# The second attention of a two-layer transformer kernel with another softmax path, another order of its steps, and batch 15's weighing shared by two engines

## The chip, the cores and the metric

One core of one Trainium2 chip runs the whole program in one launch. The metric is the device time of that launch in microseconds (us). The engines are PE (TensorE: matmuls and transposes, results to PSUM), DVE (VectorE), ACT (ScalarE), POOL (GpSimd) and SP (SyncE, which here issues DMAs).

## The reference

16 batches of 100 tokens, 512 features. Two layers, each a cross-attention and a feed-forward part, every one behind a layer norm and added to its input. The change touches only the second layer's attention and the layer norm behind it:

```python
def _L1_xattn_ref(q, latent_kv, Wq, Wkv_expand, Wout):      # 16 heads of 32
    qp = q @ Wq.T
    k, v = jnp.split(latent_kv @ Wkv_expand.T, 2, axis=-1)  # latent_kv: 100 rows, 128 wide
    scores = einsum('bhqd,bhkd->bhqk', qh, kh) / sqrt(32)
    scores = where(tril, scores, lowest)                     # causal
    attn = softmax(scores, axis=-1)
    return (einsum('bhqk,bhkd->bhqd', attn, vh) -> [b, q, 512]) @ Wout.T

x = x + _L1_xattn_ref(_layernorm(x), ctx, ...)
x = x + _L1_ffn_ref(_layernorm(x), ...)                      # 32 experts, 8 chosen per token
```

The expert part reads the normed rows twice: as transposed halves for the gate's logits, and from a table in DRAM out of which tokens are gathered.

## The kernel before, in words

The program runs stage by stage: first attention, first feed-forward part, second attention (`attention1`), routing, experts. Products keep float32 accuracy by splitting each operand into a float16 high part (written by ACT) and the rest (a float16 low part, written by DVE), and summing three products; so nearly every PSUM tile is read by ACT, then by DVE, and only then is its bank free.

`attention1` is written out by hand, engine by engine, as a loop over steps `s` (`LAST` = 22). Step `s` scores batch `s` (16 heads of 100 x 100, in four PSUM banks `sbank`, one for each head group `j`; a group is the four heads 4m + j), and finishes batch `b = s - 2`: transpose of its probabilities (`turn`, line 1880), their split (`probs_high` on ACT, line 2018, `probs_low` on DVE, line 2178), and their product with the values (`values`, line 1893). Beside it run the projections for coming batches (`project_v`, `project_qk`, line 1831, four batches or a *chunk* at a time), the output projection of a finished chunk (`output`, line 1831 with `aT`,`w_o`), its transpose back to rows (`output_rows`, line 1909), its addition to `x` (`add_rows`, line 2194), the next layer norm (`moments` line 187, `before_root`, `root` on ACT line 240, `after_root`, `norm_row` line 247, `norm_turn` line 1917, `norm_high` line 2044, `norm_low` line 2206), the rows for the gather table (`row_high` on ACT, line 2040, `row_low` on POOL, line 2108, a DMA from SP, line 1815, through two buffers) and the gate's `logit_sums`. `choose` (from line 2243) waits for the last of these.

The softmax of batch `s`: DVE takes the maxima of all 16 heads from PSUM (`peaks`, line 2154, 1600 columns) and scales them (line 2157). For three of the four head groups ACT takes exp head by head, with the maximum as bias, and sums as it goes (line 2012, 12 instructions, each with one that reads the sum). For the fourth group DVE adds the maxima itself (`shift`, line 2163), ACT takes one exp of 400 columns (line 2008), DVE sums it (line 2170). DVE inverts the totals (line 2173), POOL multiplies all 1600 probabilities (`normalise`, line 2102). The scores of the next batch may overwrite a group's bank when its exps are done.

What sets the order: every engine runs its own list in program order, with waits on semaphores. Apart from the scores, all PE results go through four rotating PSUM banks `t_bank`; `bank_uses()` lists all uses in order, and a use waits until the use four places before it has been read by both of its readers. The tables `outs_at`, `norms_at` and `sums_at` say in which steps outputs, norms and logit sums come. Before, a chunk's four outputs come in two steps, two in each.

```python
for s in range(LAST):                    # before, PE
    if s < BATCH: scores(s)
    if old: turn(b, 0..3)
    ...
    project_v(s + 1); project_qk(c, i); values(b); project_qk(c, KT + i)
```

## Time and profile before

| | us |
|---|---|
| median of 3 runs | 1847.8 (1844.77 to 1849.7) |
| profiled execution, its own time | 1844.54 |
| its span on the core | 1842.9 |
| busy in the span: PE / DVE / ACT / POOL | 1606.8 / 1192.0 / 1036.1 / 611.1 |
| second attention, from the first `peaks` to `choose` | 1020.9 to 1264.6 |
| mean granted TensorE clock over the span | 0.931 |

The profiled execution is 3.3 us shorter than the median. Its span lies 1.6 us inside its time. The second attention is 13% of the span, so shares over the whole program say little of it; it has to be read by its own stretches. PEclk is the granted TensorE clock as a share of full speed; 1.0 is 2.4 GHz, 0.5 is 1.2 GHz. Durations of matmuls overlap, since PE pipelines them: the distance of two starts is what one costs.

### The profile page before, as it was taken

Reading aid. Unit: us, or ns where it says so; the run is one execution under the profiler, and the core shown is the slowest. Engines: PE = TensorE matmul, PEld = TensorE weight load, DVE = VectorE, ACT = ScalarE, POOL = GpSimd, SP = SyncE. Lnnn points to the kernel's source line nnn. Section 1 sums busy time; section 2 is a strip of 40 time slices with the busy share of each in tenths; the row PEclk is TensorE's granted clock in tenths of the full one; section 3 lists DMA queues with packets and bytes.
Section 4 is the critical chain, followed back from the end, with each engine's and each line's share of the span. In section 5 each row is a group of like instructions: output and inputs, shape, how many; then the busy total and the mean of one; then the engine's idle time right before and its main releaser. Section 6 shows DMA issues by size and latency. Waiting matters only on the chain. (4 is left out here: it accounts for less than half of the span.)

```text
span 1842.9 us, 35610 instructions
## 1 busy us (share of the span) xinstructions
PE 1606.8 (87%) x11911; PEld 998.5 (54%) x11911; DVE 1192.0 (65%) x2678; ACT 1036.1 (56%) x2563; POOL 611.1 (33%) x481
## 2 busy tenths in 40 slices
PE   4788999999999979989997777784599999999993
PEld 3655656656656545555554454553466666666661
DVE  4866797787787779688796777757633333333332
ACT  3447746746747627566574777743655555455451
POOL 4614304304304300000000222212167777777662
PEclk9789999999999989999998998776599999999996
DMA  8820120220120249787786001104356656556536
GB/s 271 285 84 9 55 75 9 62 68 10 65 65 10 69 157 333 239 280 241 227 260 227 12 2 37 36 29 114 78 108 140 150 136 140 137 129 136 131 74 225
DMA packets 143332, 226.57 MB, mean 123 GB/s; under 512 B 37857, under 2 KB 93409, under 8 KB 143032
## 3 DMA queue, kind: packets, MB, share of 16 engines
q1 hardware_dynamic: 107160, 195.90, 33.6%
q0 software_dynamic: 29344, 21.29, 7.1%
q10 hardware_dynamic: 6656, 7.11, 1.1%
q8 instruction: 105, 1.72, 0.4%
q14 instruction: 67, 0.55, 0.1%
HBM read 175.00 MB, written 98.80 MB: 149 GB/s over the span
## 5 line engine op out<-in xcount | busy, mean ns | idle before, releaser
L2751 PE MATMUL g_ps<-ring,xT 128*128 x1572 | 300.8, 327 | 1.1 <-issue 1.1
L1051 POOL TENSOR_TENSOR pr<-pr,sm 128x1444 f32<-128x1444 f32 (+1 forms) x64 | 137.3, 2145 | 385.9 <-DVE sm L1087 385.9
L2700 POOL DMA_INDIRECT acc<-rows,slot_sources x131 | 207.8, 1586 | 107.2 <-issue 78.7
L2857 DVE SCALAR_TENSOR_TENSOR hf<-sg,g_ps 128x192 f32<-128x192 f32 x131 | 46.4, 354 | 238.5 <-ACT sg L2806 206.3
L2751 PEld LDWEIGHTS g_ps<-ring,xT 128*128 128x128 f16 x1572 | 142.8, 98 | 71.9 <-issue 5.5
L2690 POOL DMA_INDIRECT xg<-xtab,slot_sources x131 | 138.0, 1054 | 81.3 <-issue 79.5
L2773 PE MATMUL d_ps<-ring,hT 128*128 x655 | 162.8, 379 | 1.6 <-ACT hT L2819 1.1
L1081 DVE TENSOR_REDUCE sm<-s_banks 128x2 f32<-128x722 f32 (+2 forms) x128 | 97.5, 762 | 67.3 <-PE s_banks L819 64.8
L973 ACT ACTIVATE pr<-s_banks,sm 128x361 f32<-128x361 f32 (+1 forms) x208 | 115.3, 563 | 30.7 <-DVE sm L1081 29.2
L876 PE MATMUL o_bank<-cT,N_hi 128*128 128x400 f16 x512 | 129.7, 335 | 0.0
L819 PE MATMUL s_banks<-kvp,qp 128*128 128x361 f16 (+1 forms) x624 | 116.9, 318 | 10.8 <-ACT pr L973 6.1
L2098 POOL MEMSET zero_row<- 128x544 f32 x1 | 0.6, 557 | 377.5 <-POOLq L1338 377.5
L2819 ACT ACTIVATE hT<-h_ps 128x384 f16<-128x384 f16 x131 | 64.3, 491 | 101.8 <-PE h_ps L2764 99.3
L849 PE MATMUL o_bank<-probsT,kvp 128*128 128x384 f16 (+5 forms) x576 | 108.2, 333 | 1.1 <-DVE probsT L1092 1.1
L1230 ACT ACTIVATE split_o<-split_f 128x512 f16<-128x512 f32 (+1 forms) x192 | 87.9, 513 | 20.6 <-DMA split_f<-in_down 12.1
L2773 PEld LDWEIGHTS d_ps<-ring,hT 128*128 128x128 f16 x655 | 63.7, 97 | 65.6 <-issue 3.4
L2102 POOL TENSOR_TENSOR pr<-pr,sm 100x1600 f32<-100x1600 f32 x16 | 45.8, 2864 | 157.5 <-DVE sm L2173 157.5
L2833 ACT ACTIVATE rows<-d_ps,xg 128x512 f32<-128x512 f32 x131 | 90.0, 687 | 13.4 <-issue 2.2
L2851 DVE COPY xT<-x_ps 128x1024 f16<-128x1024 f16 x131 | 90.6, 692 | 10.1 <-issue 6.2
L1376 PE MATMUL gate_ps<-hT_hi,wt 128*128 128x400 f16 x256 | 86.8, 339 | 11.0 <-DVE hf L1506 9.2
L1396 PE MATMUL down_ps<-hid,wt 128*128 128x400 f16 x512 | 94.5, 345 | 0.7 <-DVE hid L1511 0.7
L2723 PEld LDWEIGHTS x_ps<-ident_h,xg 128*128 128x128 f16 x1048 | 70.0, 99 | 37.5 <-DMA xg<-xtab,slot_sources 7.1
(322 smaller groups left out, 3848.1 us busy)
## 6 DMA issues: line engine op xcount, KB each, us to landing
split_f<-in_gu SPq DMA_DIRECT2D x64, 384.0 KB, 4.5
split_gu<-split_o SPq DMA_DIRECT2D x64, 384.0 KB, 3.1
ring<-split_gu SPq DMA_DIRECT2D x32, 768.0 KB
head<-in_head SPq DMA_DIRECT2D x16, 864.0 KB
tern_w<-in_tern SPq DMA_DIRECT2D x48, 256.0 KB
split_f<-in_down SPq DMA_DIRECT2D x32, 384.0 KB, 4.2
split_d<-split_o SPq DMA_DIRECT2D x32, 384.0 KB, 3.8
ring<-split_d SPq DMA_DIRECT2D x32, 256.0 KB
```

The lines of the kernel that those rows point to most:

```text
L819: last = nc.tensor.matmul(sbank[0:n, i, 0:KEYS], qp[:, a, bi, at:at + n], kvp[:, bi % 2, k].rearrange("p j d -> p (j d)")[:, 0:KEYS], star ...
L849: last = nc.tensor.matmul(ob[1][:, 0:width(s)], kvp[0:KEYT[u], bi % 2, k, u, :], pT[s % 2][0:KEYT[u], a, u, 0:width(s)], start=(j == 0), s ...
L876: op = nc.tensor.matmul(ob[m % 2][:, 0:CH], w[:, h, f], cT[:, a, :, h * SEQ:(h + 1) * SEQ], start=(t == 0), stop=(t == len(terms) - 1))
L973: nc.scalar.activation(pr[0:n, s % 3, i, :], sbank[0:n, i, 0:KEYS], ACT.Exp, bias=small[0:n, s % 3, 0, i:i + 1], accum_out=small[0:n, s % ...
L1051: nc.gpsimd.tensor_tensor(pr[:, s % 3, 0:n], pr[:, s % 3, 0:n], small[:, s % 3, 2, 0:n].unsqueeze(2).to_broadcast([P, n, KEYS]), ALU.mult) ...
L1081: nc.vector.tensor_reduce(small[0:n, s % 3, 0, first:last], sbank[0:n, first:last, 0:KEYS], AX, ALU.max, negate=True).then_inc(peak.sem, 1)
L1396: last = nc.tensor.matmul(d_ps[m % 2][:, 0:CH], core.wt[:, 2 * KT * HT // 4 + k, m * P:(m + 1) * P], hh[:, a, k, :], start=(k == 0 and a = ...
L2690: nc.gpsimd.indirect_dma_start(out=xg[:, i % NX, :], out_offset=None, in_=core.xtab[:, :], in_offset=bass.IndirectOffsetOnAxis(ap=core.sou ...
L2700: nc.gpsimd.indirect_dma_start(out=core.acc[i % NACC][:, :], out_offset=bass.IndirectOffsetOnAxis(ap=core.sources[:, i:i + 1], axis=0), in ...
L2751: last = nc.tensor.matmul(g_ps[i % 2][:, 0:2 * INTER], xT[:, i % 2, a * KT + k, :], ring(i, (2 * k + w) * 2 * INTER, 2 * INTER), start=((k ...
L2773: last = nc.tensor.matmul(d_ps[i % 2][:, :], hT[0:parts, i % 2, pair, :], ring(i, D + col * DIM, DIM, parts), start=(n == 0), stop=(n == 4))
L2851: nc.vector.tensor_copy(xT[:, i % 2], half(x_ps[i % 2], 2 * KT)).then_inc(x_copied.sem, 1)
```

## The change

**Softmax.** `peaks` still takes the maxima. DVE then writes them as two bfloat16 parts (a cast and a subtraction, 16 columns each); PE transposes the parts (`turn_tops`), ACT copies them out (`tops_out`), and PE adds them to the scores in PSUM with one 400-column matmul of 32 rows for each group (`shift`), against a table of ones made once by POOL. ACT then needs one exp for each group (4 of 400 columns, no sums). POOL adds the two halves of each row of 100 and again the two halves of that (`totals`, 800 and 400 outputs); DVE sums the last 25 (`invert`) one step later, behind `probs_low(b, 0)`. POOL weighs one step later too. For batch 15 DVE sums all 1600 columns and weighs two of the four head groups (`normalise_first`), POOL the other two.

**Order.** On PE `turn` comes before `scores`. A chunk's outputs come one in a step (the last two of chunk 2 and all of chunk 3 in twos). Norms, moments and roots follow tables. Norms 8 to 11 all stand in step 17, between the outputs of chunk 3; logit sums of chunk 2 stand in step 19, between the last norms.

**Start.** The splits of `w_o` and of the gate's weights move from the start into steps 1 to 4, the moments for the last four batches between the first projections. Some buffers now share room with others.

```diff
+OUTS = {5: ((0, 0),), 6: ((0, 1),), 7: ((0, 2),), 8: ((0, 3),), 9: ((1, 0),), 10: ((1, 1),), 11: ((1, 2),), 12: ((1, 3),),
+        13: ((2, 0),), 14: ((2, 1),), 15: ((2, 2), (2, 3)), 17: ((3, 0), (3, 1)), 18: ((3, 2), (3, 3))}
+MOMENTS = {9: 0, 13: 1, 16: 2, 18: 3}
+ROOTED = {10: 0, 13: 1, 16: 2, 18: 3}
+NORMS = {11: (0, 1), 12: (2,), 13: (3,), 14: (4, 5), 15: (6, 7), 17: (8, 9, 10, 11), 19: (12, 13), 20: (14, 15)}
+SUMS_AFTER_TURN, SUMS_LAST = {16: 0}, {18: 1, 19: 2, 21: 3}
...
+                def turn_tops(b):
+                    pe.wait_ge(parted.sem, parted.after(b))
+                    bank = take(("top", b))
+                    nc.tensor.transpose(bank[0:TOPS, 0:SEQ // 2].bitcast(BF16),
+                                        tops[:, b % 2].rearrange("p a n -> p (a n)"), core.ident_b[0:SEQ, 0:SEQ]
+                                        ).then_inc(tops_turned.sem, 1)
+
+                def shift(b):
...
+                    pe.wait_ge(tb.sem(("top", b)), tb.after(("top", b)))
+                    for j in range(HQ):
+                        nc.tensor.matmul(sbank[0:SEQ, j, 0:CH], topsT[:, b % 2, :],
+                                         select[:, j].rearrange("p m k -> p (m k)"), start=False, stop=True,
+                                         skip_group_check=True).then_inc(shifted.sem, 1)
...
                 def exps(b, j):
-                    if j == 0:
-                        act.wait_ge(scaled.sem, scaled.after(b))
...
-                    for m in range(KT):
-                        n = HQ * m + j
-                        nc.scalar.activation(pr[:, b % 3, n, :], sbank[0:SEQ, j, m * SEQ:(m + 1) * SEQ], ACT.Exp,
-                                             bias=sm[:, b % 3, 1, n:n + 1], scale=SCORE_SCALE,
-                                             accum_out=sm[:, b % 3, 2, n:n + 1]).then_inc(powered.sem, 1)
+                    act.wait_ge(shifted.sem, shifted.after(b, j + 1))
+                    nc.scalar.activation(group(pr[:, b % 3], j), sbank[0:SEQ, j, 0:CH].rearrange("p (m k) -> p m k", m=KT),
+                                         ACT.Exp, scale=SCORE_SCALE).then_inc(powered.sem, 1)
...
+                def totals(b):
+                    pool.wait_ge(powered.sem, powered.after(b))
...
+                    nc.gpsimd.tensor_tensor(halves[:, :, :], pr[:, b % 3, :, 0:SEQ // 2], pr[:, b % 3, :, SEQ // 2:SEQ], ALU.add
+                                            ).then_inc(folded.sem, 1)
+                    pool.wait_ge(folded.sem, folded.after(b, 1))
+                    nc.gpsimd.tensor_tensor(halves[:, :, 0:SEQ // 4], halves[:, :, 0:SEQ // 4], halves[:, :, SEQ // 4:SEQ // 2],
+                                            ALU.add).then_inc(folded.sem, 1)
...
                 def invert(b):
-                    dve.wait_ge(powered.sem, powered.after(b))
-                    nc.vector.tensor_reduce(own_of(sm[:, b % 3, 2, :]), own(pr[:, b % 3]), AX, ALU.add
-                                            ).then_inc(totalled.sem, 1)
+                    if b == BATCH - 1:
+                        dve.wait_ge(powered.sem, powered.after(b))
+                        nc.vector.tensor_reduce(sm[:, b % 3, 2, :], pr[:, b % 3], AX, ALU.add).then_inc(totalled.sem, 1)
+                    else:
+                        dve.wait_ge(folded.sem, folded.after(b))
+                        nc.vector.tensor_reduce(sm[:, b % 3, 2, :], halves[:, :, 0:SEQ // 4], AX, ALU.add
+                                                ).then_inc(totalled.sem, 1)
```

The order on DVE, in a step with outputs, before (the `peaks` of step 7 to the outputs of that step, and the next `peaks`):

```order
L2154 TENSOR_REDUCE sm<-s_banks 100x16
L2157 TENSOR_SCALAR sm<-sm 100x16
L2163 TENSOR_TENSOR pr<-s_banks,sm 100x4x100
L2178 TENSOR_TENSOR pT<-t_bank,pT 100x4x100 x4
L2170 TENSOR_REDUCE sm<-pr 100x4
L2173 RECIPROCAL sm<-sm 100x16
L2146 SCALAR_TENSOR_TENSOR v<-t_bank,v 100x512
L2140 SCALAR_TENSOR_TENSOR qT<-t_bank,qT 128x400
L2186 TENSOR_TENSOR aT<-t_bank,aT 128x4x100
L2140 SCALAR_TENSOR_TENSOR kT<-t_bank,kT 128x400
L2194 SCALAR_TENSOR_TENSOR x_rows<-t_bank,x_rows 100x4x128 x2
L2154 TENSOR_REDUCE sm<-s_banks 100x16
```

and in the changed kernel (line numbers are its own; L2200 is `peaks`, L2203 and L2205 the two parts, L2214 the sum of POOL's folds, L2245 `add_rows`, L2229 `probs_low`):

```order
L2200 TENSOR_REDUCE sm<-s_banks 100x16
L2203 CAST peak_parts<-sm 100x16
L2205 TENSOR_TENSOR peak_parts<-sm,peak_parts 100x16
L2194 SCALAR_TENSOR_TENSOR v<-t_bank,v 100x512
L2188 SCALAR_TENSOR_TENSOR qT<-t_bank,qT 128x400
L2237 TENSOR_TENSOR aT<-t_bank,aT 128x4x100
L2188 SCALAR_TENSOR_TENSOR kT<-t_bank,kT 128x400
L2245 SCALAR_TENSOR_TENSOR x_rows<-t_bank,x_rows 100x4x128
L2229 TENSOR_TENSOR pT<-t_bank,pT 100x4x100
L2214 TENSOR_REDUCE sm<-half_sums 100x16
L2217 RECIPROCAL sm<-sm 100x16
L2229 TENSOR_TENSOR pT<-t_bank,pT 100x4x100 x3
```

`peaks` comes last in a step's softmax work instead of first, one `add_rows` stands where two stood, and the sum of a batch is taken in the step after its exps.

The order on PE in the changed kernel, in such a step (L1893 `turn`, L1865 the scores, L1873 `turn_tops`, L1906 `values`, L1882 `shift`; the rows of the query projection, L1828 with `w_q`, are the dots):

```order
L1893 MATMUL t_bank<-ident,pr 100x100 x16
L1858 MATMUL s_banks<-causal,ident_b 100x400 x4
L1865 MATMUL s_banks<-kT,qT 100x100 x48
L1828 MATMUL t_bank<-w_kv,lat 100x512 x3
...
L1873 MATMUL t_bank<-ident_b,peak_parts 32x100
L1906 MATMUL t_bank<-pT,v 32x100 x48
L1882 MATMUL s_banks<-head_select,peak_parts_T 100x400 x4
L1828 MATMUL t_bank<-aT,w_o 128x400 x12
L1828 MATMUL t_bank<-lat,w_kv 128x400 x3
L1922 MATMUL t_bank<-ident,oT 100x128 x4
```

Two kinds of instruction are new on PE, between the query projection and the outputs. The order on ACT behind batch 15's probabilities, before:

```order
L2033 ACTIVATE oT<-t_bank 128x400 x2
L2040 ACTIVATE row_parts<-ln_h 100x512
L2044 ACTIVATE hT_hi<-t_bank 128x4x100
L2040 ACTIVATE row_parts<-ln_h 100x512
L2044 ACTIVATE hT_hi<-t_bank 128x4x100
L2033 ACTIVATE oT<-t_bank 128x400 x2
```

and now (L2052 copies outputs, L2059 is `row_high`, L2063 `norm_high`):

```order
L2052 ACTIVATE oT<-t_bank 128x400 x2
L2059 ACTIVATE row_parts<-w_f 100x512
L2063 ACTIVATE hT_hi<-t_bank 128x4x100
L2059 ACTIVATE row_parts<-w_f 100x512
L2063 ACTIVATE hT_hi<-t_bank 128x4x100
L2059 ACTIVATE row_parts<-w_f 100x512
L2063 ACTIVATE hT_hi<-t_bank 128x4x100
L2059 ACTIVATE row_parts<-w_f 100x512
L2063 ACTIVATE hT_hi<-t_bank 128x4x100
L2052 ACTIVATE oT<-t_bank 128x400 x2
```

Four rows and four norms stand between the two pairs of outputs of chunk 3, where two of each stood.

## Rows read from the trace of the kernel before

**Rows 1.** Busy time by stretch (us; PE, PEld, DVE, ACT, POOL; granted clock, DMA)

```profile
1020.90:1069.70 48.80, 36.39 (x555) 21.95 (x554) 33.84 (x61) 36.48 (x158) 14.01 (x5) 0.93 0.01 2
...
1079.80:1094.80 15.00, 12.34 (x168) 7.88 (x168) 8.61 (x16) 8.73 (x35) 3.13 (x2) 1.00 0.01 1
1094.80:1113.70 18.90, 15.26 (x182) 9.70 (x181) 12.48 (x27) 10.36 (x37) 2.86 (x1) 0.91 0.11 35
...
1171.70:1182.40 10.70, 7.50 (x116) 5.30 (x117) 8.90 (x20) 10.18 (x37) 2.23 (x1) 0.57 0.05 18
...
1206.90:1264.60 57.70, 45.03 (x512) 34.90 (x511) 32.44 (x75) 23.89 (x64) 9.72 (x7) 0.74 0.15 47
```

**Rows 2.** Waits, 1000 to 1290: total us, times, longest

```profile
POOL pr L2102 <- DVE sm L2173: 157.5, 16, 23.4
...
PEld t_bank L1831 <- DVE pT L2178: 33.8, 15, 5.1
DVE sm L2170 <- ACT pr L2008: 32.2, 16, 4.0
```

**Rows 3.** Timeline of step 4, all engines: start, duration, engine, line

```profile
1059.54 1.58 PE L1880 MATMUL t_bank<-ident,pr 100*100 100x100 f32 x16
1059.66 1.82 DVE L2154 TENSOR_REDUCE sm<-s_banks 100x16 f32<-100x1600 f32 x1 [1.22 <-PE s_banks L1870]
1060.12 1.69 ACT L2018 ACTIVATE pT<-t_bank 100x400 f16<-100x400 f32 x4 [2.38 <-PE t_bank L1880]
...
1062.09 2.01 DVE L2178 TENSOR_TENSOR pT<-t_bank,pT 100x400 f16<-100x400 f32 x4
...
1066.20 0.57 DVE L2170 TENSOR_REDUCE sm<-pr 100x4 f32<-100x400 f32 x1 [1.66 <-ACT pr L2008]
...
1068.13 0.84 PE L1863 MATMUL s_banks<-causal,ident_b 100*100 100x400 bf16 x4
...
1069.71 1.82 DVE L2154 TENSOR_REDUCE sm<-s_banks 100x16 f32<-100x1600 f32 x1 [0.18 <-PE s_banks L1870]
```

**Rows 4.** POOL's weighing, group by form

```profile
L2102 POOL TENSOR_TENSOR pr<-pr,sm 100x1600 f32<-100x1600 f32 x16 | 45.8, 2864 | 157.5 <-DVE sm L2173 157.5
```

**Rows 5.** Timeline: outputs at clock 1.0 and lower, rows added, moments, table load

```profile
1108.24 1.28 ACT L240 ACT_TABLE_LOAD   x1
...
1109.78 2.47 DVE L187 BATCH_NORM_STATS2 ln3c_st<-x_rows 100x6 f32<-100x512 f32 x4
...
1145.84 4.22 PE L1831 MATMUL t_bank<-aT,w_o 128*128 128x400 f16 x24 [0.92 <-DVE v L2146]
...
1150.53 1.49 DVE L2194 SCALAR_TENSOR_TENSOR x_rows<-t_bank,x_rows 100x512 f32<-100x512 f32 x2 [3.40 <-PE t_bank L1909]
...
1212.57 6.65 PE L1831 MATMUL t_bank<-aT,w_o 128*128 128x400 f16 x24
```

**Rows 6.** Timeline: a small DVE instruction beside none, and beside POOL's

```profile
1173.52 0.17 DVE L2157 TENSOR_SCALAR sm<-sm 100x16 f32<-100x16 f32 x1
...
1182.99 2.27 POOL L2108 TENSOR_TENSOR row_parts<-ln_h,row_parts 100x512 f16<-100x512 f32 x2
...
1184.28 1.02 DVE L2157 TENSOR_SCALAR sm<-sm 100x16 f32<-100x16 f32 x1
```

**Rows 7.** Timeline of the end of the stage; first and last of 48 logit products

```profile
1237.47 6.14 PE L1831 MATMUL t_bank<-aT,w_o 128*128 128x400 f16 x24 [1.26 <-issue]
...
1256.92 1.92 DVE L247 TENSOR_SCALAR ln_h<-x_rows,ln3c_t 100x512 f32<-100x512 f32 x4
...
1260.25 0.23 PE L1831 MATMUL s_banks<-gate_w,hT_hi 128*100 128x32 f16 x1
...
1264.30 0.25 PE L1831 MATMUL s_banks<-gate_w,hT_hi 128*100 128x32 f16 x1
...
1264.59 1.67 DVE L2243 MAX8 gate_top<-s_banks 100x8 f32<-100x32 f32 x16 [2.99 <-PE s_banks L1831]
```

**Rows 8.** SP's waits, 1100 to 1290: the landing of the last table row

```profile
SPq L1820 <- DMA xtab<-row_parts: 2.7, 1, 2.7
```

More of the change, by code:

```diff
@@ L1637 @@
 HQ = HEADS // KT
-OWN = HQ - 1
 LAG = 2
@@ L1961, in _ @@
                         project_qk(c, i)
+                    if s < BATCH:
+                        turn_tops(s)
                     if old:
                         values(b)
-                    if c < NCH:
+                    if s < BATCH:
+                        shift(s)
+                    if c < NCH and keys_first(s):
+                        project_qk(c, KT + i)
+                    for k, m in outs_at(s):
+                        pe.wait_ge(w_lo, KT + 3)
+                        output(k, m)
+                    if c < NCH and not keys_first(s):
                         project_qk(c, KT + i)
@@ L2072, in _ @@
                         attended_high(b)
-                    if c < NCH:
+                    if s < BATCH:
+                        for j in range(HQ):
+                            exps(s, j)
+                    if c < NCH and keys_first(s):
+                        qk_high(c, KT + i)
+                    for k, m in outs_at(s):
+                        copy_out(k, m)
+                    if c < NCH and not keys_first(s):
                         qk_high(c, KT + i)
@@ L2266, in choose, with all_added @@
                     ts(core.mask, cutp[:, :, :], 1.5 * LOWEST, None, ALU.is_lt)
+                def all_added(k):
+                    for n in range(KT):
+                        dve.wait_ge(tb.sem(("rows", k, n)), tb.after(("rows", k, n)))
                 for j in range(QK):
                     qk_low(0, j)
+                    if j < CB:
+                        ln2.moments(dve, BATCH - CB + j, j)
                 v_low(0)
-                ln2.after_root(dve, 0)
+                ln2.before_root(dve, 0)
                 for s in range(LAST):
```

264 lines of the change are left out of this document (141 added, 123 removed).

## The prediction

> **What bounds the kernel now.** I read the table of busy time by stretch first, cut at the starts of `peaks`. In it the second attention lasts 243.7 us: 186.0 from the first `peaks` (1020.9) to that of batch 15 (1206.9), and 57.7 from there to `choose` [rows 1]. No engine is full: in the step 1079.8 to 1094.8 PE is busy 12.3 of 15.0 us, DVE 8.6, ACT 8.7. So the steps are bound by waits, and I read those next: POOL idles for DVE's reciprocal, PE waits 33.8 us for `probs_low` to free a bank, DVE waits 32.2 us for the exps of its own group [rows 2]. The timeline of step 4 shows the ring behind it: `peaks` at 1059.66, 12 exps and the group's exp until 1066.2, where DVE sums, then the projections' splits, scores at 1068.13, the next `peaks` at 1069.71 [rows 3]. That is 10.05 us. A step with two outputs costs 15.0 and one that also takes moments 18.9 [rows 1], since both outputs stand between two `peaks`. ACT's exps are on that ring, and that is what the change attacks.
>
> **Prices.** Distances of starts: a group's transposes 1.58/4, so 0.35; one `probs_high` 0.42 and one `probs_low` 0.5 (four in 1.69 and 2.01); `peaks` 1.82; a sum of 400 columns with the reciprocal 0.85 [rows 3]. Twelve output matmuls are half of 24 in 4.22, so 2.05; two `add_rows` take 1.49, so 0.7 each; moments 2.5, the seven small instructions behind them 0.2 each, an activation table 1.28 [rows 5]. POOL's 1600 columns take 2.86 [rows 4], so its folds of 800 and 400 take 1.43 and 0.72. New forms: an exp of 400 columns from PSUM lies between `probs_high` (0.42) and the 0.32 of a 100-column exp times four; I take 0.43, the nearest in columns, bounds 0.4 to 0.6. A shift matmul has the 400 columns of an output matmul: 0.17 (bounds 0.15 to 0.35, the lower clock). The cast and the subtraction cost as line 2157: 0.2 each [rows 6], upper bound 1.0. The transpose of the maxima and ACT's copy: 0.1 and 0.25, with handovers 0.6.
>
> **A step with one output**, placed by hand, time from its first transpose, PE at full clock. PE: transposes to 1.4, scores to 2.95, values' and queries' projections to 5.7, then a wait. DVE: first `probs_low` 1.1 to 1.6, `invert` to 2.45, three `probs_low` to 3.95, `peaks` to 5.8, parts to 6.2. PE turns them; ACT's copy is out at 6.75. `values` to 7.2, shift 7.3 to 8.0, ACT exps 7.85 to 9.75. Output to 10.05, keys to 10.55, output copied by 10.75, rows to 11.3. DVE: key split to 11.8, `add_rows` to 12.5. Only then comes the next step's first `probs_low` (to 12.95), `invert` (its folds are ready at 12.0), three more, and `peaks` at 15.35. Period 15.35 - 3.95 = **11.4 us**. ACT saves about 2.5 us a step, but its exps are no longer on the ring there: PE's line from the maxima to the rows is, and PE is busy 10.4 of 11.4.
>
> **A step without output**: exps end at 9.75, POOL's folds at 12.0, `invert` 12.05 to 12.9, three `probs_low`, `peaks` at 14.4. Period **10.5**, against 10.05 now: the relief of ACT is paid back as folds that DVE waits for ahead of `peaks`.
>
> **The 15 periods.** Steps 0 to 4: 9.0 (no transposes, but the folds), 11.5 and 11.0 (1.0 for the cast behind POOL, see below; 0.5 for the late `w_o` splits on ACT), 10.5, 10.5. Step 5 (output and a layer-norm transpose) 11.8, steps 6 to 8 11.4 each, step 9 11.75 (its moments fit into DVE's idle time), step 10 12.15 (a table load), step 11 14.1 (table load 1.28, two rows and two norms on ACT between output and `probs_high`), step 12 11.8, step 13 12.9 (moments and root), step 14 13.65. Sum 174.85 against 186.0: **-11.15**. The gain comes from steps 6, 7, 10 and 11 (before 15.0, 18.9, 15.0, 18.9).
>
> **The start**: the first `peaks` now has the value split and seven small instructions ahead of it, but `w_o` no longer: 1021.4 against 1020.9, **+0.5**. The maxima table that POOL makes (four copies of 400 columns of 32 rows, at most 0.72 each) is hidden by the projections; without them it would cost 3 us.
>
> **The end**, from batch 15's `peaks` to `choose`, before 57.7. Outputs 2 and 3 of chunk 2, norms 6 and 7 and their `add_rows` end at 12.9; `probs_low`, the full sum of batch 15 (1.85 and 0.25), two multiplications of 400 columns on DVE beside 800 on POOL, three `probs_low`, values of batch 14 at 19.8. Then moments and small instructions (3.9) stand before the root, and ACT's list has the root before batch 15's `probs_high`: values of 15 at 28.6. Two outputs at the lower clock, 6.1 [rows 7], to 36.8. Then four rows and four norms on ACT, 1.05 each; row 10 must also wait until row 8 has landed: 0.6 for its high part, 1.2 for POOL's (half of 2.27 [rows 6]), 2.7 to land [rows 8], that is 2.9 us more than ACT's own line. The banks of the next two outputs come free with norms 10 and 11. Those outputs, at the lower clock again for the first, rows, `add_rows`: 52.2. Moments, root: 3.9 and 0.3, then 1.2 of small instructions: norm rows at 57.4. Before, norm rows to `choose` took 7.7 [rows 7]; now chunk 2's logit sums (48 products, 4.05 at that clock [rows 7]) stand between the last norms: 10.5. Sum 67.9: **+10.2**. Not tested by any row is whether PE falls to the lower clock there; at full clock the three places give back 5.
>
> **Weighing a rule.** A 16-column DVE instruction took 0.17 alone and 1.02 beside POOL's row work, ending when POOL did [rows 6]; the sum of step 1 and batch 15's multiplications are charged with such waits, 1.0 and 1.4. The Trainium skill (SBUF — State Buffer, "Who interferes with whom") says why: casts and tensor_scalar in a two-port mode, and instructions with two SBUF inputs, contend with GpSimd for an exclusive lock held for the whole instruction. By this rule the trace's 1.02 is no accident and sums (tensor_reduce) stay free; by it the total is the same unless POOL's 2.86 us moves later, which is the third rival.
>
> **Sum.** +0.5 - 11.15 + 10.2 = -0.45. The profiled execution took 1844.5, so 1844.1 in its terms; it stood 3.3 under the median of 1847.8, so **1847.3**. I call 0.3% (5.5 us, about the 4.9 between lowest and highest of three runs) the least that a measurement tells from none: 1842.3 to 1853.3.
>
> **Rivals.**
> (a) *PE keeps its clock and the end does not stretch: faster.* Against: stretches with PE waiting 2 to 5 us show 0.57 to 0.93 [rows 1]. For: the new steps leave PE only 1 us idle in 11.4, and 1079.8 to 1094.8, with PE busy 82%, shows 1.00. Then the end gives back 5, and the steps with small gaps run 0.5 shorter in eleven of fifteen cases: -0.45 - 5 - 5.5 = -11, 1836.
> (b) *PE falls to the lower clock in the last five steps: slower.* Steps 12 to 15 have no projections, PE waits 2.5 us for the maxima there, and the same steps before ran at 0.57 [rows 1]; 10.7 us long, since PE was not on their ring. Now first transposes, `values`, shift, output and rows (0.35 + 0.7 + 0.7 + 2.05 + 0.5 = 4.3) are. By 6.65 against 4.22 for 24 matmuls [rows 5] that is +58%, 2.5 us a step. It decides from three steps on: +7.5, 1855; in five, 1860.
> (c) *POOL's weighing reaches `peaks`.* POOL has to end 0.4 us before the cast. If its folds or the row work start it 1 us later, the cast and all behind it wait: 0.6 us in ten steps, +6, 1853.5.
>
> **How the numbers follow.** The forecast, that the gain of the steps is given back at the end, 0.42. Rival (a), 0.32: the order of the steps was worked at full clock already, but the end has 5 us of clock in it. Rival (b) 0.16, (c) 0.10. Within the forecast the unknown prices (an exp of 0.6 instead of 0.43 is +0.7 on each of four steps; the clock) put 0.03 beyond the band on either side; (a) puts 0.31 on the faster side and 0.01 in the band, (b) 0.15 slower and 0.01 in it, (c) 0.08 and 0.02. Faster 0.34, same 0.40, slower 0.26. The range takes (a) and some of its bounds, and (b) at five steps: 1831 to 1860.
>
> **What would show it.** In the timeline of the changed kernel: `peaks` starts 11.4 apart in steps 6 to 9 and 10.5 in steps 2 to 5 (above 12 speaks for (b) or (c)); PE's wait ahead of the transpose of maxima of 0.5 in steps 6 to 9; the cast after `peaks` 0.2 long (0.8 or more is (c)); batch 15's `peaks` at 1196.2; `choose` at 1264.1; a wait of ACT's row 10 for a DMA of about 3 us; the clock in the four steps before batch 15's `peaks`. The prediction fails if the steps with output take 10 or less, or the end takes under 62.

## The result, and the profile after

| | before | after |
|---|---|---|
| median, us | 1846.11 (20 runs, 1840.24 to 1849.70) | 1849.84 (20 runs, 1844.68 to 1854.54) |
| profiled execution, its own time | 1844.54 | 1853.64 |
| first `peaks` to that of batch 15 | 186.0 | 175.9 |
| batch 15's `peaks` to `choose` | 57.7 | 72.2 |
| second attention, POOL's `zero_row` to `choose` | 260.2 | 265.7 |

The ratio is 1.0024, with a 95% interval of 1.0015 to 1.0033: the changed kernel is slower by 0.24%, some 4.4 us (the two medians differ by 3.7), where 1847.3 and no net gain or loss were forecast (its own sum said -0.45 us). The time lies inside the 0.3% band and inside the range, yet the interval is clear of 1: a small loss that was not forecast. The profiled execution of after stands 3.8 us above its median; its stages ahead of the second attention, where nothing was changed, are 5.5 us later than in the profile of before. So what follows compares the stage with the stage. In the repeat below the stage takes 265.8 us, and its 15 periods agree with these within 0.1 us each.

The busy time by stretch of the changed kernel, cut at the starts of `peaks` (columns as in [rows 1]; the first line is step 6, then steps 12 and 13, then the end):

```profile
1090.67:1101.73 11.06, 10.72 (x156) 6.76 (x155) 7.60 (x15) 6.09 (x14) 5.40 (x4) 1.00 0.01 1
...
1160.56:1174.91 14.35, 11.68 (x145) 7.01 (x144) 7.49 (x16) 6.34 (x14) 6.55 (x5) 0.76 0.08 25
1174.91:1189.39 14.48, 10.70 (x145) 6.36 (x144) 11.75 (x26) 7.91 (x17) 6.54 (x5) 0.88 0.14 41
...
1203.41:1275.60 72.19, 50.05 (x509) 36.82 (x509) 35.21 (x77) 21.67 (x44) 12.65 (x10) 0.69 0.14 43
```

A step with one output takes 11.06 us, and PE is busy for 10.72 of them: PE is the bound there now. Before, 15.0 and 18.9 us went to a step with two [rows 1]. Its waits, 1000 to 1290 (columns as in [rows 2]), show where they moved:

```profile
POOL half_sums L2132 <- ACT pr L2032: 76.4, 15, 19.4
...
ACT peak_parts_T L2027 <- PE t_bank L1873: 36.6, 16, 3.9
...
POOL pr L2146 <- DVE sm L2217: 22.3, 15, 2.5
...
PE t_bank L1873 <- DVE peak_parts L2205: 14.9, 12, 2.9
```

DVE's 32.2 us of waiting for its own group's exps [rows 2] are gone; the 33.8 of PE's weight loads for `probs_low` have fallen to 1.8. A new wait is PE's for the parts of the maxima (line 2205), 14.9 us in all, of which 9.9 fall in steps 12 to 15. The timeline of step 7 shows the new ring, which answers to [rows 3]:

```profile
1101.73 1.81 DVE L2200 TENSOR_REDUCE sm<-s_banks 100x16 f32<-100x1600 f32 x1
1103.58 0.17 DVE L2203 CAST peak_parts<-sm 100x16 bf16<-100x16 f32 x1
...
1104.02 0.22 PE L1873 MATMUL t_bank<-ident_b,peak_parts 100*32 100x100 bf16 x1
...
1104.98 0.87 PE L1882 MATMUL s_banks<-head_select,peak_parts_T 32*100 32x400 bf16 x4
...
1105.50 1.68 ACT L2032 ACTIVATE pr<-s_banks 100x400 f32<-100x400 f32 x4
1105.79 2.20 PE L1828 MATMUL t_bank<-aT,w_o 128*128 128x400 f16 x12
...
1107.26 1.63 POOL L2132 TENSOR_TENSOR half_sums<-pr 100x800 f32<-100x800 f32 x1 [3.89 <-ACT pr L2032]
1108.96 0.91 POOL L2135 TENSOR_TENSOR half_sums<-half_sums 100x400 f32<-100x400 f32 x1
...
1110.65 0.56 DVE L2214 TENSOR_REDUCE sm<-half_sums 100x16 f32<-100x400 f32 x1
...
1112.80 1.81 DVE L2200 TENSOR_REDUCE sm<-s_banks 100x16 f32<-100x1600 f32 x1
```

The maxima go through PE in 0.22 and 0.87 us, the four exps take 1.68, POOL's folds end at 1109.87, and DVE sums at 1110.65: the softmax works as the change means it to, and the cast took 0.17 us, clear of POOL. Only in step 1 did it take longer, 1.26 us (from 1039.01 to 1040.27), until POOL's weighing of 1037.38 to 1040.24 was over.

Where the time comes back is seen from step 12 on. In the timeline of the changed kernel, steps 12 and 13 and then the end of the stage:

```profile
1162.85 0.26 PE L1873 MATMUL t_bank<-ident_b,peak_parts 100*32 100x100 bf16 x1 [2.08 <-DVE peak_parts L2205]
...
1165.79 3.91 PE L1828 MATMUL t_bank<-aT,w_o 128*128 128x400 f16 x12
...
1182.25 0.81 DVE L218 TENSOR_TENSOR ln3c_t<-ln3c_st 100x4 f32<-100x4 f32 x1
...
1184.83 1.28 ACT L240 ACT_TABLE_LOAD   x1
...
1186.12 0.20 ACT L240 ACTIVATE ln3c_t<-ln3c_t 100x4 f32<-100x4 f32 x1
1186.23 1.67 ACT L2037 ACTIVATE pT<-t_bank 100x400 f16<-100x400 f32 x4
...
1205.69 0.22 PE L1873 MATMUL t_bank<-ident_b,peak_parts 100*32 100x100 bf16 x1 [2.86 <-DVE peak_parts L2205]
...
1208.01 7.00 PE L1828 MATMUL t_bank<-aT,w_o 128*128 128x400 f16 x24
...
1221.71 2.39 DVE L2223 TENSOR_TENSOR pr<-pr,sm 100x400 f32<-100x400 f32 x2
...
1221.76 1.91 POOL L2143 TENSOR_TENSOR pr<-pr,sm 100x800 f32<-100x800 f32 x1 [3.33 <-DVE sm L2217]
...
1248.14 0.63 ACT L2059 ACTIVATE row_parts<-w_f 100x512 f16<-100x512 f32 x1 [2.53 <-DMA xtab<-row_parts]
...
1249.92 6.52 PE L1828 MATMUL t_bank<-aT,w_o 128*128 128x400 f16 x24 [2.94 <-DVE hT_lo L2257]
...
1264.35 1.60 PE L1930 MATMUL t_bank<-ident,w_f 100*128 100x100 f32 x8 [4.47 <-DVE w_f L247]
...
1269.89 1.58 PE L1930 MATMUL t_bank<-ident,w_f 100*128 100x100 f32 x8
```

Five places stand out. PE waits 2.08 us for the maxima in step 12, where no projection fills the time, and its 12 outputs then take 3.91 us instead of 2.20 in step 7. Cut finer, the granted clock is 1.00 up to 1162, 0.50 from 1163 to 1168, and 1.00 again from 1170: it falls towards the end of that wait. PE waits 2.86 us for them in step 15, whose 24 outputs then take 7.00, against 4.22 at full clock [rows 5]. DVE and POOL weigh batch 15 side by side for 2.39 and 1.91 us. ACT waits 2.53 us until row 8's DMA has landed, and PE 2.94 behind it. The last two norm turns come 5.54 us after the two before them, with chunk 2's logit sums between.

### The profile page after: what moved, and what is told of

The parts are those of the page before. It is cut to its first block and busy times, and to the rows that moved or that the text cites. A ratio compares the mean times of both kernels' runs of the same rounds, so it can differ in the third digit from the quotient of the medians.

```text
span 1851.9 us, 35540 instructions
## 1 busy us (share of the span) xinstructions
PE 1621.8 (88%) x11991; PEld 1002.9 (54%) x11991; DVE 1191.9 (64%) x2681; ACT 996.7 (54%) x2244; POOL 652.1 (35%) x516
## 5 line engine op out<-in xcount | busy, mean ns | idle before, releaser
L2812 PEld LDWEIGHTS g_ps<-ring,xT 128*128 128x128 f16 x1572 | 142.2, 98 | 71.9 <-issue 6.3
L1230 ACT ACTIVATE split_o<-split_f 128x512 f16<-128x512 f32 (+1 forms) x192 | 88.0, 513 | 22.3 <-DMA split_f<-in_down 13.1
L1376 PE MATMUL gate_ps<-hT_hi,wt 128*128 128x400 f16 x256 | 86.1, 336 | 11.6 <-DVE hf L1506 9.8
L2784 PE MATMUL x_ps<-ident_h,xg 128*128 128x128 f16 x1048 | 80.7, 220 | 6.4 <-DMA xg<-xtab,slot_sources 6.4
```

Of the source, the lines that this page charges most:

```text
L2784: last = nc.tensor.transpose(half(x_ps[i % 2], 2 * KT)[:, k, :], parts[:, k * P:(k + 1) * P], core.ident_h[:, :])
L2812: last = nc.tensor.matmul(g_ps[i % 2][:, 0:2 * INTER], xT[:, i % 2, a * KT + k, :], ring(i, (2 * k + w) * 2 * INTER, 2 * INTER), start=((k ...
```

## The experiments

Every run's stage is measured in its profile: the sum of the 15 periods, and the end from batch 15's `peaks` to `choose`. The times are medians; the ratios are to the kernel before on the same chip, and runs of different chips are compared by their ratios. Each edit is made to the changed kernel. Line numbers in a run's rows are its own.

**A repeat of the changed kernel.** No edit.

> The changed kernel again, as the measure for the runs beside it. Theory A (order and clock, both inside the second attention): the stage repeats, within 1 us: 175.9 us from the first score maxima to those of batch 15, 72.2 from there to the first MAX8, against 186.0 and 57.7 before; time 3 to 5 us above before. Rival R (the loss is an accident of the profiled run, whose earlier stages were 5.5 us late): one of the two stretches differs by 3 us or more, and the times stand within 1 us of before.

1849.2 us, 1.0023 [1.0013, 1.0033], periods 175.9, end 72.2. The stage is reproducible; the loss is real.

**PE filled in steps 12 to 15.** Twelve matmuls of 400 columns whose results nothing uses (the bank's part that the transpose doesn't need).

```diff
                 def turn_tops(b):
-                    pe.wait_ge(parted.sem, parted.after(b))
                     bank = take(("top", b))
+                    if b >= 12:
+                        for _ in range(12):
+                            nc.tensor.matmul(bank[0:SEQ, 64:464], ...)
+                    pe.wait_ge(parted.sem, parted.after(b))
```

> In steps 12 to 15 PE runs 12 extra matmuls of 400 columns into an unused part of the bank of the maxima while it waits for them (no result uses them); nothing else moves. Theory A, clock part: PE's idle time there drops the granted clock, so filling it brings the 12 output matmuls of step 12 from 3.9 us back to 2.2, and the periods of steps 12, 13 from 14.35 and 14.5 to about 12 and 13; the outputs of step 15 from 7.0 to 4.2. In sum 6 to 8 us off the stage. Rival (DVE or POOL set those periods): the periods stay within 0.5 us, whatever the clock shows, or grow by the extra work.

1845.35 us, 1.0004 [0.9987, 1.0020]; periods 174.8, end 69.7. PE in the timeline of step 12:

```profile
1158.60 2.19 PE L1874 MATMUL t_bank<-causal,ident_b 100*100 100x400 bf16 x12
1160.84 0.22 PE L1878 MATMUL t_bank<-ident_b,peak_parts 100*32 100x100 bf16 x1
...
1162.61 2.20 PE L1828 MATMUL t_bank<-aT,w_o 128*128 128x400 f16 x12
```

The step falls from 14.35 to 11.47, and 12 outputs take 2.20 instead of 3.91. The only thing put in was work, so the 2.9 us were the clock's. In step 15 the 24 outputs took 4.23 instead of 7.00, and the values of batch 14 come 3.3 us sooner behind the `peaks`; the two pairs of chunk 3 then took 6.61 and 6.80 instead of 6.08 and 6.52, so that the end is only 2.5 shorter.

Step 13 stayed at 14.47 though its 12 outputs took 2.19 instead of 3.87. The rows of the two kernels show why. In the changed kernel the root (1186.12) stands on ACT's list behind the copy of the slow outputs, a row, a norm and the table load (1184.83); DVE had finished what the root needs at 1184.26, so the 0.81 us beside POOL's fold cost nothing there. With the outputs at full clock ACT comes sooner, and DVE's small instructions, two of which take 0.82 and 1.08 us beside POOL's fold and row work instead of 0.17, are what comes last:

```profile
1177.36 0.82 DVE L218 TENSOR_TENSOR ln3c_t<-ln3c_st 100x4 f32<-100x4 f32 x1
1178.21 1.08 DVE L219 TENSOR_TENSOR ln3c_t<-ln3c_st 100x4 f32<-100x4 f32 x1
...
1181.05 1.06 PE L1898 MATMUL t_bank<-ident,pr 100*100 100x100 f32 x8 [2.35 <-DVE hT_lo L2262]
```

PE waits 2.35 us behind them (0.35 in the changed kernel). Two chains of nearly the same length stand in that step; no run removed the second one.

Not all of the clock came back: steps 2 to 4 took 10.54, 10.84 and 10.90 instead of 10.33 to 10.35, with a clock of 0.72 in step 3, and each of steps 5 to 11 took 0.1 to 0.2 longer, perhaps for the new order of PE's two waits. The stage is 262.2 us, 3.5 under the changed kernel and 2.0 over before. Expected were 6 to 8 off.

**Moments, root and norms of chunk 2 as early as before.**

```diff
-MOMENTS = {9: 0, 13: 1, 16: 2, 18: 3}
+MOMENTS = {9: 0, 13: 1, 15: 2, 18: 3}
-NORMS = {..., 15: (6, 7), 17: (8, 9, 10, 11), 19: (12, 13), 20: (14, 15)}
+NORMS = {..., 15: (6, 7), 16: (8, 9), 17: (10, 11), 19: (12, 13), 20: (14, 15)}
```

(`ROOTED` likewise.)

> Moments and root of chunk 2 go back into step 15, norms 8 and 9 into step 16, 10 and 11 into step 17, as before the change; logit sums, batch 15's weighing and all earlier steps stay. Theory A, order part: the wait of row 10 for its DMA (2.5 us) goes, and the outputs of chunk 3 follow each other sooner; the end shrinks from 72.2 to 64 to 67. Rival (the end is long for the clock alone): it stays above 70, since PE waits as before.

1847.55 us, 1.0013 [0.9998, 1.0028]. End 69.0, 3.2 less and short of what was expected. The moments now stand ahead of batch 14's `probs_low` on DVE, and PE waits 8.53 us for the latter instead of 3.69. The wait for row 10's DMA is gone, PE waits 0.64 instead of 2.94 ahead of the last pair of outputs, and that pair takes 4.22 instead of 6.52. (Step 15's outputs took 5.42 instead of 7.00, which the edit doesn't explain.) The periods are 178.9, though nothing ahead of step 15 was edited. Steps 12 to 14 in its table of stretches:

```profile
1159.19:1173.23 14.04, 12.41 (x147) 7.43 (x147) 7.49 (x14) 6.13 (x14) 5.56 (x5) 0.76 0.06 17
1173.23:1188.35 15.12, 12.10 (x145) 7.04 (x144) 11.86 (x26) 8.01 (x17) 6.55 (x5) 0.77 0.13 40
1188.35:1203.43 15.08, 11.19 (x145) 6.99 (x145) 9.34 (x22) 7.97 (x17) 7.68 (x6) 0.77 0.19 59
```

Steps 13 and 14 have a clock of 0.77 where the changed kernel has 0.88, and 0.6 to 1.1 us more. The clock falls at other places without any change to the work there.

**DVE sums batches 0 to 4 itself.** POOL's folds go in those steps, DVE sums 1600 columns instead of 400.

```diff
-                    if b == BATCH - 1:
+                    if b == BATCH - 1 or b < 5:
```

> For batches 0 to 4 DVE sums all 1600 columns itself, as it does for batch 15, and POOL folds nothing for them. Theory A: in steps without output the ring runs through POOL's folds (2.2 us), so a sum of 1.8 instead of folds and 0.57 makes the periods of steps 1 to 4 shorter by about 1.0 (from 10.3 to 9.4), 4 to 5 us in all. Rival (DVE is the fuller engine, and POOL's relief is worth it): they grow by up to 1.2 each, since DVE does 1.25 us more in every step.

1851.36 us, 1.0032 [1.0018, 1.0045]; periods 178.9, end 71.9. Steps 1 to 4 took 11.62, 11.55 (at a clock of 0.71), 10.74, 10.73 against 10.84, 10.33, 10.33, 10.35; step 0 took 9.12 against 9.68. They were expected to get shorter by 1.0 each; the rival came. The wait of `invert` went, and 1.25 us more of DVE work came in its place ahead of `peaks`. So POOL's folds pay for themselves in steps 1 to 4, even where DVE waits for them.

**Logit sums of chunk 2 behind those of chunk 1.**

```diff
-SUMS_AFTER_TURN, SUMS_LAST = {16: 0}, {18: 1, 19: 2, 21: 3}
+SUMS_AFTER_TURN, SUMS_LAST = {16: 0}, {18: (1, 2), 21: (3,)}
```

> Edit: the logit sums of chunk 2 stand directly behind those of chunk 1, ahead of the last four norm turns, not between the turns of rows 12, 13 and those of rows 14, 15. In the changed kernel the last two norm turns come 5.5 us after the two before them (1264.35 and 1269.89) and ACT and DVE wait 4.3 us there. Theory (that list order costs the end 2.5 to 4 us): batch 15's maxima to the choice goes from 72.2 to 68 to 69.5, the 15 periods stay 175.9 +- 0.2, the kernel gets 2.5 to 4 us shorter. Rival (PE is the bound there whatever the order: the sums come later or earlier by the same 4 us, and the norm rows wait for them): 72.2 +- 0.5. Rival 2 (chunk 2's norms are not copied out yet when chunk 1's sums end, so PE waits for them ahead of chunk 3's outputs): end 73 to 75.

1845.58 us, 1.0008 [0.9993, 1.0023]; periods 175.9, end 68.05: 4.1 less. PE's line now has the four norm turns in one:

```profile
1263.80 2.93 PE L1930 MATMUL t_bank<-ident,w_f 100*128 100x100 f32 x16 [1.78 <-DVE w_f L247]
```

The sums run in PE's wait for the moments (4.47 us in the changed kernel, 1.78 now). The place in the list was the whole cost.

**POOL weighs all of batch 15.** DVE's two multiplications go; DVE still sums.

```diff
-                    if b == BATCH - 1:
-                        late = pr[:, b % 3].rearrange("p (m j) k -> p m j k", j=HQ)[:, :, HQ // 2:HQ, :]
...
-                        return
...
-                    if s == BATCH:
-                        normalise_first(BATCH - 1)
```

> Edit: POOL weighs all four groups of batch 15 (1600 columns) and DVE none; DVE still sums that batch. In the changed kernel DVE's two groups took 2.39 us for two beside POOL's 800 columns in 1.91, and the three probs_low of batch 14 came behind them, values of 14 at 1225.7. Theory (the split of batch 15 between DVE and POOL costs more than it gives, both hold each other up): values of 14 come 1.5 to 2.4 us earlier, POOL's 2.9 us are over before batch 15's turn is due, and the end goes from 72.2 to 70 to 70.7. Rival (the root and its row of norms stand ahead of probs_high of batch 15 on ACT, so an earlier values(14) brings nothing): 72.2 +- 0.4. Rival 2 (POOL's 2.9 us slow the small instructions of DVE ahead of the root): 73 to 74. Periods 175.9 +- 0.2 in all three.

1845.59 us, 0.9994 [0.9979, 1.0009]; periods 175.9, end 68.95: 3.2 less, more than expected. DVE, PE and POOL there:

```profile
1218.77 0.25 DVE L2209 RECIPROCAL sm<-sm 100x16 f32<-100x16 f32 x1
1218.94 1.47 DVE L2221 TENSOR_TENSOR pT<-t_bank,pT 100x400 f16<-100x400 f32 x3
...
1219.11 2.86 POOL L2138 TENSOR_TENSOR pr<-pr,sm 100x1600 f32<-100x1600 f32 x1 [3.33 <-DVE sm L2209]
...
1220.56 0.71 PE L1904 MATMUL t_bank<-pT,v 100*32 100x100 f16 x48 [1.21 <-DVE pT L2221]
1222.02 2.90 PE L1891 MATMUL t_bank<-ident,pr 100*100 100x100 f32 x16 [0.75 <-POOL pr L2138]
```

`probs_low` starts right behind the reciprocal, not 2.6 us behind it (1221.42 and 1224.02 in the changed kernel), and PE waits 1.21 instead of 3.69 for it. POOL's 1600 columns took 2.86 beside `probs_low`, which reads PSUM and SBUF: no stretch on either side. PE then waits 0.75 for POOL, all that the split had to win. Sharing the batch cost 3.2 us. How much of it is the two engines holding each other up, and how much the work that DVE no longer does ahead of `probs_low`, is not separated: no run has DVE's two products without POOL beside them. Two `probs_low` of the same 400 columns take 1.04 us, and by that estimate 1.3 of the 2.39 would be the holding up.

**Rows 10 and 11 later.**

```diff
                     for n in norms_at(s):
-                        if n < BATCH - CB:
+                        if n < BATCH - CB - 2:
                             row_high(n)
                         norm_high(n)
...
+                    if s == BATCH + LAG:
+                        row_high(10)
+                        row_high(11)
```

> Edit: the high parts of rows 10 and 11 are taken by ACT after it has copied the first two outputs of chunk 3, and not ahead of them, between norms 8, 9 and 10, 11. In the changed kernel ACT waits 2.53 us for row 10's DMA, and PE's outputs of chunk 3 (second pair) wait 2.94 us for a bank. Theory (ACT's wait for the DMA of row 10 holds up norms 10, 11 and with them the banks): the second pair of outputs starts 2 to 3 us earlier, the end goes from 72.2 to 69 to 70. Rival (the outputs wait for something else at the same time, the DMA wait is idle time that comes back at the next hand-over): 72.2 +- 0.5. Rival 2 (rows 10, 11 are then late for the norms behind them): 73 to 74. Periods 175.9 +- 0.2.

1843.7 us, 0.9995 [0.9980, 1.0011]; periods 179.0 (the pattern of the run with early moments, with 15.13 and 15.06 in the same two steps), end 66.0: 6.2 less. Its second pair of outputs:

```profile
1248.00 1.29 ACT L2063 ACTIVATE hT_hi<-t_bank 128x400 f16<-128x400 f32 x3
...
1249.74 4.22 PE L1828 MATMUL t_bank<-aT,w_o 128*128 128x400 f16 x24
```

The wait of 2.94 us is gone, as expected. What was not expected: PE, which has no gap ahead of them any more, makes these outputs at full clock, 4.22 instead of 6.52, as it did in the run with early moments. The wait cost its length and 2.3 us of clock behind it, 5.2 of the 6.2. The rest is not explained by the edit: step 15's outputs, ahead of it, took 5.40 instead of 7.00, and the first pair of chunk 3 6.95 instead of 6.08.

**Outputs in pairs as before**, all else as in the changed kernel.

```diff
-OUTS = {5: ((0, 0),), 6: ((0, 1),), 7: ((0, 2),), 8: ((0, 3),), 9: ((1, 0),), ...
+OUTS = {6: ((0, 0), (0, 1)), 7: ((0, 2), (0, 3)), 10: ((1, 0), (1, 1)), 11: ((1, 2), (1, 3)), 14: ((2, 0), (2, 1)), ...
```

> Edit: the outputs of chunks 0 to 2 are made two in a step (steps 6, 7, 10, 11, 14, 15) as in the kernel before, everything else as in the changed kernel. Theory (the gain of the 15 periods, 186.0 to 175.9, comes mostly from the outputs being spread one a step, since PE's line from the maxima to the rows is the ring, and not from the shorter exps): steps without output 10.3 to 10.6, steps with two 14 to 17, the 15 periods 182 to 188. Rival (the redesigned exps gain as well with two outputs in a step, since DVE's idle time before took the output): steps with two 12.5 to 13.5, sum 172 to 177.

1857.21 us, 1.0075 [1.0047, 1.0104]; periods 184.6, end 70.5. A step with two outputs and the one behind it:

```profile
1097.58:1111.36 13.78, 13.16 (x171) 8.39 (x170) 8.19 (x17) 6.83 (x15) 5.39 (x4) 1.00 0.08 22
1111.36:1121.69 10.33, 9.13 (x145) 5.69 (x144) 7.09 (x14) 5.99 (x14) 5.40 (x4) 1.00 0.15 53
```

So putting the outputs back in pairs costs 8.7 of the 10.1 us that the periods win. The other 1.4 are what all the rest of the change leaves over in these periods: exps, folds, the order on PE and the moved moments and norms, which no run takes apart. That sum hides larger ones. In steps 6, 7, 10 and 11 the changed kernel takes 20.6 us off (67.8 to 47.3), and the kernel with pairs still takes 10.5 off (57.4), partly because the moments have left steps 7 and 11; in steps 12 to 14 both give back 7.6 and 8.9, and in steps 0 to 4 some 2.7.

**The three edits of the end together** (logit sums, POOL for batch 15, late rows).

> Edit: the three edits of the end together, as each ran alone: logit sums of chunk 2 directly behind those of chunk 1, POOL weighs all of batch 15, the high parts of rows 10 and 11 behind ACT's copies of chunk 3's first outputs. Alone they took the end from 72.2 to 68.1, 69.0 and 66.0, that is -4.1, -3.2 and -6.2. Theory (they stand at different places of the end, so they add): end 58.5 to 60, the whole stage 252 to 256, kernel 5 to 8 us shorter than before (ratio 0.996 to 0.997). Rival (they overlap: POOL's lateness behind row 8 is what both the second and the third relieve): end 62 to 64, kernel within 0.2% of before. The 15 periods are 175.9 or 179.0, the two sums seen so far in kernels that are alike there.

1837.46 us, 0.9959 [0.9945, 0.9973]; periods 175.9, end 58.9. 72.2 - 4.1 - 3.2 - 6.2 = 58.7: they add. (Here too step 15's outputs took 5.40, as in the run with late rows, so some of the 6.2 is in both for a reason that is not known.) The end is within 1.2 us of where it stood before the change (57.7), with the periods' gain kept. The stage is 252.7, 7.6 under before, as much as the ratio says.

**The same, and PE filled at two places**: ahead of the maxima of batches 12 to 15 as above, and ten matmuls ahead of the values of batches 14 and 15.

> Edit: as the three together, and PE runs matmuls whose results nothing uses in its waits: 12 of 400 columns ahead of the transpose of the maxima of batches 12 to 15, 10 ahead of the values of batches 14 and 15. Theory (PE's lower clock in steps 12 to 15 and behind the two waits of the end is worth 1.5 to 2.9 us a place): step 12 11.5 and the last 15 periods 3 us less than without the filling, the 24 output matmuls behind the values of batch 15 take 4.3 to 5.5 us instead of 7.0, end 2 to 4 us below that of the three together, kernel 4 to 7 us below it. Rival (the end is bound by ACT, DVE and the DMA, not by PE's clock): end the same within 0.7 us, kernel 1 to 3 us below it.

1833.53 us, 0.9934 [0.9915, 0.9954]; periods 174.2. Steps 12 to 14 gained 3.4 us as expected (step 12: 11.46), while step 5 took 13.28 instead of 11.6; the end was 60.8, not 2 to 4 below 58.9, and the outputs behind batch 15's values took 5.76 (4.3 to 5.5 expected). In its timeline:

```profile
1212.73 3.55 PE L1907 MATMUL t_bank<-causal,ident_b 100*100 100x400 bf16 x10
...
1223.71 3.57 PE L1907 MATMUL t_bank<-causal,ident_b 100*100 100x400 bf16 x10 [3.47 <-DVE pT L2236]
```

Each ten run at the lower clock, and the second ten start only after PE's wait of 3.47 us for `probs_low`, which stands at the bank ahead of them: they fill nothing and stand on the path themselves. The stage is 252.3, against 252.7 without the filling, so the 3.9 us between the medians are not shown to be its work.

**The same filling at both places, with early moments instead of late rows.**

> Edit: the same filling, the logit sums of chunk 2 behind those of chunk 1, POOL for all of batch 15, but moments, root and norms of chunk 2 as early as in the kernel before (moments in step 15, norms 8 and 9 in step 16, 10 and 11 in step 17) in place of the late high parts of rows 10 and 11. Theory (early norms are the fuller remedy, since the rows' DMA wait falls in time that is idle anyway): end 1 to 3 us below that of the three together with the filling. Rival (moments ahead of batch 15's sum delay its probabilities, and what row 10 saved comes back there): end 0 to 3 us above it.

1834.12 us, 0.9937 [0.9918, 0.9956]; periods 172.3, end 59.5; all outputs of chunks 2 and 3 at full clock. The end is 1.3 below the run before it, as expected, and the medians don't tell the two apart: they are two remedies for one wait.

**The three edits, filled ahead of the maxima only.**

> Edit: the three edits of the end together, and the filling only ahead of the transpose of the maxima of batches 12 to 15, not ahead of the values of 14 and 15. With the filling at both places the four-step stretch 12 to 15 shortened by 3.4 us and chunk 2's 24 output matmuls in step 15 took 4.23 us, but the end was 60.8 against 58.9 without any filling: ten matmuls ran at the lower clock ahead of each values, 3.55 us each. Theory (those two fillings delay the values they stand ahead of and win less behind them): end 56.5 to 58 (58.9 less up to 2.8 from chunk 2's outputs), 15 periods 172.0 to 172.8 where no early step falls to the lower clock, kernel 1831 to 1834, ratio to before 0.992 to 0.994. Rival (chunk 2's outputs are not on the end's chain, which goes over batch 14's and 15's probabilities): end 58.9 +- 0.5, ratio 0.994 to 0.996.

1828.98 us, 0.9910 [0.9893, 0.9926]: the fastest median of the study, 0.9% faster than before, and 1.1% faster than the changed kernel by the two ratios. Its end is 56.3, its periods 175.3. Steps 5 and 12 and the end:

```profile
1073.42:1086.67 13.25, 12.00 (x157) 7.38 (x155) 8.64 (x18) 5.69 (x14) 5.40 (x4) 0.87 0.01 3
...
1156.55:1168.01 11.46, 10.83 (x157) 7.31 (x156) 7.48 (x15) 6.24 (x14) 6.51 (x5) 1.00 0.10 31
...
1197.05:1253.39 56.34, 45.29 (x521) 35.48 (x521) 32.59 (x75) 21.45 (x44) 12.72 (x10) 0.77 0.18 56
```

The end fell by 2.6, a little more than expected; the periods missed their 172.0 to 172.8, since step 5 ran at 0.87 and took 13.25 instead of 11.6. The stage is 248.7, 11.6 under before; the medians differ by 16.7. The rest of the kernel, 575.1 us from `choose` on against 578.3 before, accounts for 3.2 more. What is left over, about 2 us, is no more than the executions scatter ahead of the stage.

## Why the prediction was right or wrong

**The step that failed.** The sum took PE at full clock in steps 12 to 15, where PE waits for the maxima with no projections to run. Its terms were 11.8, 12.9 and 13.65 us for steps 12 to 14 and 12.9 for the first mark of the end. Measured were 14.35, 14.48, 14.02 and 15.8, with PE's 12 outputs at 3.91, 3.87 and 3.64 instead of 2.20 and its 24 at 7.00 instead of 4.22. With the waits filled step 12 fell to 11.47 and step 15's outputs to 4.23. A second, smaller term was mis-sized: the logit sums between the last norms, 2.8 in the sum, cost 4.2.

**What bounds the kernel, and the ring.** Right. The gain was to come from steps 6, 7, 10 and 11, and came there: 18.8 us forecast, 20.6 measured. The run with pairs shows that spreading the outputs is worth 8.7 over the 15 periods. In step 7 PE does not wait for the maxima at all (0.5 forecast); the cast took 0.17.

**Steps 0 to 11.** 136.5 us forecast (52.5 and 84.0), 133.0 measured. Step 2: 11.0 forecast, steps 3 and 4: 10.5, measured 10.33 to 10.35; steps 6 to 8: 11.4, 11.06; step 11: 14.1, 13.2. The working was sound, and most terms were a little long. The exp of 400 columns cost 0.42 (1.68/4), where 0.43 was taken. POOL's folds took 1.63 and 0.91 and not 1.43 and 0.72 by the price of the weighing; that was hidden in the steps with outputs, while in steps 0, 1, 3 and 4 DVE waited 3.6 us in all for the folds.

**Steps 12 to 14.** 38.35 forecast, 42.85 measured, +4.5. Rival (b) had named the mechanism (no projections, 2.5 us of waiting, the outputs on the ring; the waits were 2.08, 2.08, 2.84 and 2.86), but it was kept out of the sum at 0.16. By the filling the clock was worth 2.9 us in step 12 and 0.45 in step 14. In step 13 the slow outputs are on the chain that ends last, and another chain, over DVE's small instructions beside POOL, is as long: the step stays at 14.5 when the clock is given back. That second chain was not in the sum either. That the 15 periods came out at 175.9 with 174.85 forecast is luck: -3.5 and +4.5 stand behind it.

**The start.** +1.15 instead of +0.5. The table that POOL makes was said to be hidden by the projections; it runs beside DVE's split of `w_q` ahead of them, in the timeline of after:

```profile
1010.56 3.45 DVE L2168 SCALAR_TENSOR_TENSOR w_q<-w_f,w_q 128x512 f16<-128x512 f32 x4 [3.02 <-ACT w_q L2001]
1010.66 3.72 POOL L2125 COPY head_select<-head_of 32x400 bf16<-32x400 bf16 x4
```

The split took 2.50 before, and the next one, of `w_kv`, 1.53 instead of 1.23. By the rule of the Trainium skill that the prediction weighed (SBUF — State Buffer, "Who interferes with whom"), this is the lock again, and the trace agrees: the four splits with two SBUF inputs took 0.95 us longer.

**The end.** 67.9 forecast, 72.2 measured; +14.5 over before, not +10.2. Its order of events was right, two of its terms were too small. Against the forecast's own marks, counted from batch 15's `peaks`:

| mark | forecast | measured |
|---|---|---|
| chunk 2's last `add_rows` ends | 12.9 | 15.8 |
| values of batch 14 | 19.8 | 22.3 |
| values of batch 15 | 28.6 | 31.3 |
| first two outputs of chunk 3 end | 36.8 | 39.8 |
| norm rows 12 to 15 start | 57.4 | 60.3 |
| `choose` | 67.9 | 72.2 |

2.9 us enter at the first mark and are carried: step 15's outputs took 7.00. They start 4.6 us behind `peaks` and end 4.2 ahead of the mark, so the forecast's 12.9 has room only for outputs at full clock. From the first mark to the norm rows 44.5 us were forecast and 44.6 measured, each mark's distance within 0.4: there the waits that were priced (batch 15's contention, the DMA of row 8, the low-clock outputs of chunk 3) were right. The last mark adds 1.4: the logit sums between the norms cost 4.1 in all, as their removal shows, where the sum had 2.8. The forecast that "at full clock the three places give back 5" is borne out only in part: chunk 3's two pairs of outputs took 1.9 and 2.3 less in the run with filling and early moments (4.22 each); the third place, step 15, gave back 2.8 with the filling, but that was never in the 67.9.

**The sum.** +0.65 (start) - 3.5 (steps 0 to 11) + 4.5 (steps 12 to 14) + 4.3 (end) = +5.95 on the stage over the forecast of -0.45, the 5.5 that the profiles show. The lower clock in steps 12 to 15 accounts for 2.55 + 1.6 + 0.35 + 2.9 = 7.4 of it (step 13's 1.6 has the second cause beside it), the logit sums for 1.4; the faster early steps and the slower start take off 2.9. The run with filling gave back 5.8 in steps 12, 14 and the end, and lost 2.3 in other steps; it stands at 1.0004. The rest of the kernel was 2.0 shorter in the profile after, which no term had.

**The rivals.** (a) needed PE to keep its clock and the end not to stretch. The clock was 1.00 from step 2 to step 11, and those steps were shorter than the sum; the end stretched. (b) is what happened, at a lower price: the clock fell in all four of steps 12 to 15 (the text speaks of five), and cost 2.9, nothing by itself, 0.45 and 3.3 us, where 2.5 each were said. That is 6.6 against the 7.5 of its three steps, and the early steps took half of it back; so the time is not 1855. (c) came in step 1 alone, where the sum had charged it. The prediction's test, that it fails with periods under 10 or an end under 62, did not strike; it watched the steps with projections and the end as a whole, not the clock of steps 12 to 15.

## What to carry to other kernels

When a wait is put on an engine's critical line where there is nothing else to run (the last steps of a loop, without the projections), price what stands behind it at the lower clock too: here waits of 2.1 to 2.9 us stood ahead of outputs that took 1.7 and 2.8 us more, and matmuls nobody reads, run inside the wait, brought it back in steps 12 and 15. It brought nothing where a second chain was as long (step 13), and cost time where the matmuls stood behind the wait. A change that gains in the steady part and moves work to the end should have its end measured by itself: three edits there, two of list order and one of which engine does a product, took 13.3 us off without taking any arithmetic away. Two engines sharing one batch of two-input SBUF products can be slower than one of them doing it alone.
